# Low-rank weight products as two half-height matmuls side by side, a gate spread in rounded parts, and a few moved instructions

## What is computed

```python
mod = (silu(c) @ wmod).reshape(2, 6, 1, 512)
sa, ca, ga, sb, cb, gb = (mod[:, i] for i in range(6))
ga, gb = (sign(g) * maximum(abs(g), 0.25) for g in (ga, gb))
h = layernorm(x) * (1 + ca) + sa
x = x + ga * (h @ (weight * block_mask).T + bias)
h = layernorm(x) * (1 + cb) + sb
lin = lambda v, w, a, b: v @ w.T + (v @ a.T) @ b.T * 2.0     # rank 16
g = silu(lin(h, w1, A1, B1)) * lin(h, w3, A3, B3)            # hidden 1376
x = x + gb * lin(g, w2, A2, B2)
```

## Time and profile before

| | |
|---|---|
| time, median of 3 runs | 249.12 us (248.8 to 249.45) |
| the profiled execution: its time, its span | 249.18 us, 247.4 us |
| granted TensorE clock, mean | 0.999 of full |
| busy: PE, DVE, ACT, POOL | 239.4, 150.2, 94.6, 40.6 us |

### The profile page before, as it was taken

How to read it: one execution, slowest core, us unless ns; L and a number is a source line. 1 busy time by engine, 2 the same in 40 slices (tenths; PEclk the granted TensorE clock), 3 DMA queues, 4 the chain that set the end, 5 groups by cost and what they waited for, 6 DMA issues and landing times.

```text
span 247.4 us, 3423 instructions
## 1 busy us (share of the span) xinstructions
PE 239.4 (97%) x1205; PEld 187.3 (76%) x1205; DVE 150.2 (61%) x258; ACT 94.6 (38%) x174; POOL 40.6 (16%) x57
## 2 busy tenths in 40 slices
PE   7899899999999999999999999999999999999993
PEld 5567566777778888888888778888888888888772
DVE  2778699989989768855654514745454245424524
ACT  2365388957443231646456212113121212122210
POOL 2002477412101033033032000340000000000000
PEclk9999999999999999999999999999999999999999
DMA  5999999502242342231233550040000000000005
GB/s 132 367 400 389 389 404 388 172 28 85 96 132 71 86 120 53 86 124 44 87 115 65 46 33 0 17 153 3 0 1 0 0 3 0 0 0 3 0 0 170
DMA packets 14565, 26.37 MB, mean 107 GB/s; under 512 B 1618, under 2 KB 3538, under 8 KB 14420
## 3 DMA queue, kind: packets, MB, share of 16 engines
q1 hardware_dynamic: 14112, 26.01, 33.2%
q10 hardware_dynamic: 436, 0.15, 0.2%
HBM read 23.26 MB, written 2.10 MB: 103 GB/s over the span
## 4 chain that ended last, share of the span: by engine, by line
PE 84%; DVE 8%; DMA 2%; issue 1%; ACT 1%; POOL 0%; SPq 0%; DVEq 0%; POOLq 0%; ACTq 0%
PE up_a L1346 17%; PE up_b L1346 16%; PE acc L1372 8%; PE up_a L1355 8%; PE acc L1374 8%; PE acc L1373 8%; PE up_b L1355 8%; PE acc L1300 3%; DMA wa<-in_weight 2%; PE side L1328 2%; DVE stats L816 2%; PE side L1300 2%; DVE wa_lo L918 1%; DVE xt L1006 1%; PE side L1333 1%
## 5 line engine op out<-in xcount | busy, mean ns | idle before, releaser
L1095 DVE TENSOR_TENSOR g<-up_b,g 128x512 f32<-128x512 f32 (+1 forms) x22 | 15.2, 690 | 43.2 <-PE up_b L1355 43.2
L1372 PE MATMUL acc<-w_hi,g_hi 128*128 128x512 f32 (+1 forms) x88 | 34.9, 397 | 0.0
L1374 PE MATMUL acc<-w_hi,g_lo 128*128 128x512 f32 (+1 forms) x88 | 34.8, 395 | 0.0
L1373 PE MATMUL acc<-w_lo,g_hi 128*128 128x512 f32 (+1 forms) x88 | 34.7, 395 | 0.0
L791 ACT ACTIVATE g_hi<-g 128x512 fp32r<-128x512 f32 (+1 forms) x22 | 13.9, 632 | 51.2 <-DVE g L1095 51.2
L976 DVE SCALAR_TENSOR_TENSOR raw<-side,raw 128x512 f32<-128x512 f32 (+2 forms) x31 | 20.2, 677 | 19.1 <-PE side L1328 11.4
L722 ACT ACTIVATE w_hi<-raw 128x512 fp32r<-128x512 f32 (+2 forms) x33 | 20.3, 625 | 17.2 <-DVE raw L976 17.2
L781 ACT ACTIVATE g<-up_a 128x512 f32<-128x512 f32 (+1 forms) x22 | 13.1, 597 | 33.0 <-PE up_a L1355 33.0
L1346 PE MATMUL up_a<-ht_hi,w_hi 128*128 128x512 f32 (+1 forms) x88 | 24.7, 401 | 0.3 <-ACT w_hi L722 0.3
L1346 PE MATMUL up_b<-ht_hi,w_hi 128*128 128x512 f32 (+1 forms) x88 | 23.8, 393 | 0.0
L1355 PE MATMUL up_b<-ht_lo,w_hi 128*128 128x512 f32 (+1 forms) x88 | 23.8, 392 | 0.0
(11 more groups left out here) (162 smaller groups left out, 340.6 us busy)
## 6 DMA issues: line engine op xcount, KB each, us to landing
raw<-in_ffn SPq DMA_DIRECT2D x33, 256.0 KB, 2.7
xt<-in_x SPq DMA_DIRECT2D x8, 256.0 KB, 10.8
wmod_sb<-in_wmod SPq DMA_DIRECT2D x2, 1024.0 KB, 13.8
wmod_sb<-in_wmod SPq DMA_DIRECT2D x1, 2048.0 KB, 14.6
out<-xt SPq DMA_DIRECT2D x8, 256.0 KB, 2.5
mask_sb<-in_mask SPq DMA_DIRECT2D x4, 256.0 KB, 6.5
ca_sb<-in_wmod_ca SPq DMA_DIRECT2D x4, 256.0 KB, 6.4
wa<-in_weight SPq DMA_DIRECT2D x4, 256.0 KB, 6.7
```

The lines of the kernel that those rows point to most:

```text
L1095: nc.vector.tensor_tensor(g[0:w], up_b[0:w], g[0:w], ALU.mult).then_inc(g_ready, 1)
L1372: nc.tensor.matmul(acc[t][:], hi, down_hi[j][0:w], start=(j == 0), stop=False)
L1373: nc.tensor.matmul(acc[t][:], hi, down_lo[j][0:w], start=False, stop=False)
L1374: last = nc.tensor.matmul(acc[t][:], lo, down_hi[j][0:w], start=False, stop=(j == HT - 1))
```

## The change

It has four parts.

1. An up piece is now one weight over all features. `merge_up(j)` issues eight matmuls for a slice: for each of four feature slices k one over rows 0 to 63 of `parts` (w1) and one over rows 64 to 127 (w3), 128 columns each, into two banks. `spread`, `b13` and `half_on` are gone. `up_high(s, n)` waits for piece n alone.
2. The gate of batch 0 stands in two rows of each group (`c` is sent with a third row that repeats the first). ACT rounds the gates (`gate_high`), DVE turns the second row into the remainder (`gate_split`), and `spread_gate` is four single-pass matmuls with `select`.
3. DVE's `columns_sa` stands ahead of `masked_weight_low(1, 2)`. On POOL `x_low(1)` stands ahead of the first `root`; `x_low(2)` and `x_low(3)` wait for the gates instead of `norm_cols_ready`.
4. On PE `spread_gate`, `mod_rows_f` and `columns_f` stand two matmuls (`attend` of one k and m) later, and the two first merges are one `merge_up(0)` ahead of `attend(1, 3, 0, last_two)`.

```diff
-            def spread(j):
...
-                    nc.gpsimd.tensor_scalar(b13[:, n, 0:w],
-                                            f32(parts[:, LORA_B13 + j * P:LORA_B13 + j * P + w]),
-                                            half_on[:, n:n + 1], None, ALU.mult).then_inc(b13_ready, 1)
...
             x_low(0)
+            x_low(1)
             root(NORM_A[0], slice(0, T))
 
-            pool.wait_ge(norm_cols_ready, 1)
-            for k in range(1, KT):
-                x_low(k)
-            spread(0)
+            pool.wait_ge(gates_ready, 1)
+            x_low(2)
+            x_low(3)
...
+            def gate_high():
+                act.wait_ge(gates_ready, 1)
+                nc.scalar.activation(gate_parts[:], gates_a[:], ACT.Copy).then_inc(gate_high_ready, 1)
...
             row_sum(0)
+            gate_high()
             row_sum(1)
...
+            def gate_split():
+
+                dve.wait_ge(gate_high_ready, 1)
+                nc.vector.scalar_tensor_tensor(gate_parts[:], f32(gate_parts[:]), const[:, KEEP_GATE:KEEP_GATE + 1],
+                                               gates_a[:], ALU.mult, ALU.add).then_inc(gate_parts_ready, 1)
...
+            columns_sa()
             masked_weight_low(1, 2)
...
-            columns_sa()
...
             gates_of(0)
+            gate_split()
             masked_weight_low(1, 3)
...
-                    pe.wait_ge(b13_ready, 2 * (j + 1))
-                    for k in range(KT // 2):
-                        at = LORA_A13 + (n * KT // 2 + k) * P
-                        last = nc.tensor.matmul(dst[:, k * 2 * w:(k + 1) * 2 * w], parts[:, at:at + P],
-                                                b13[:, :, 0:w], start=True, stop=True)
...
+                for k in range(KT):
+                    at = LORA_A13 + k * P
+                    for n in range(2):
+                        rows = slice(n * RANKS, (n + 1) * RANKS)
+                        last = nc.tensor.matmul(merge_bank(PIECE[j, n])[:, k * w:(k + 1) * w], parts[rows, at:at + P],
+                                                parts[rows, b:b + w], start=True, stop=True)
+                        if k == KT - 1:
+                            last.then_inc(merge_out, 1)
...
-                pe.wait_ge(w_high_ready, PIECE[j, 1] + 1)
+                pe.wait_ge(w_high_ready, PIECE[j, n] + 1)
...
+            attend(1, 3, 0, first)
             spread_gate()
-            attend(1, 3, 0, first)
...
-            for at in pieces_up(s):
-                merge(PIECE[at])
+                if pieces_up(s):
+                    merge_up(s + 1)
```

More of the change, by code:

```diff
@@ L318, in build @@
         x1_by_dve = sem("x1_by_dve")
-        b13_ready = sem("b13_ready")
         merge_out = sem("merge_out")
@@ L1182, in columns_ca @@
                     pe.wait_ge(ca_ready, k)
-                nc.tensor.matmul(acc[2][:, k * B:(k + 1) * B], mod_rows[:, 0:P], ct[:, KT], start=True, stop=True
+                nc.tensor.matmul(acc[2][:, k * B:(k + 1) * B], mod_rows[:, 0:P], ct[:, KT, 0:B], start=True, stop=True
                                  ).then_inc(ca_cols_out, 1)
@@ new lines, in merge_up @@
+                    for n in range(2):
+                        free_side(("merge", PIECE[j, n]))
+                pe.wait_ge(parts_ready, 2 if j < 2 else 3)
+                b = LORA_B13 + j * P
+                for k in range(KT):
+                    at = LORA_A13 + k * P
+                    for n in range(2):
+                        rows = slice(n * RANKS, (n + 1) * RANKS)
[3 more added lines that the diff above has]
+                            last.then_inc(merge_out, 1)
@@ L1336, in up_high, with merge_down @@
+            def merge_down(r):
+                j, _ = PIECES[r]
+                w = WIDTH[j]
+                free_side(("merge", r))
+                pe.wait_ge(parts_ready, 4 if j < 2 else len(LORA_CUTS))
+                at, b2 = LORA_A2 + (j // 2) * P, LORA_B2 + j % 2 * D
+                nc.tensor.matmul(merge_bank(r)[0:w], parts[:, at:at + w], parts[:, b2:b2 + D], start=True, stop=True
+                                 ).then_inc(merge_out, 1)
             def up_high(s, n, dst):
@@ L1354, in up_rest @@
                         pe.wait_ge(low_by_dve, k + 1)
-                    last = nc.tensor.matmul(dst[0:w], up_hi[j][:, k, n], ht_lo[b][:, k],
+                    last = nc.tensor.matmul(dst[0:w], up_hi[j][:, n, k], ht_lo[b][:, k],
                                             start=False, stop=(k == KT - 1))
@@ L1424, in _ @@
                 attend(1, 0, m, last_two)
+            attend(1, 1, 0, last_two)
             mod_rows_f()
-            for m in range(3):
+            for m in range(1, 3):
                 attend(1, 1, m, last_two)
+            attend(1, 2, 0, last_two)
             columns_f()
-            pe.wait_ge(parts_ready, 2)
-            merge(0)
-            for m in range(3):
+            for m in range(1, 3):
                 attend(1, 2, m, last_two)
+            merge_up(0)
             attend(1, 3, 0, last_two)
-            merge(1)
             attend(1, 3, 1, last_two)
@@ L1462, in _ @@
                         down(0, t)
-                    merge(PIECE[piece_mid(s)])
+                    merge_down(PIECE[piece_mid(s)])
                 if s:
@@ L1472, in _ @@
                 elif s == 1:
-                    merge(PIECE[piece_late(s)])
+                    merge_down(PIECE[piece_late(s)])
                 else:
@@ L1492, in launch_inputs @@
     for j, w in enumerate(WIDTH):
-        both = np.stack([by_feature(up[j * P:j * P + w].T) for up in (w1, w3)], axis=2)
+        both = np.stack([by_feature(up[j * P:j * P + w].T) for up in (w1, w3)], axis=1)
         for n in range(2):
@@ L1514, in launch_inputs @@
     consts[:, KEEP_A] = -(p // R % 2)
-    for n in range(2):
-        consts[:, HALF_ON + n] = p // RANKS == n
     for q in range(KT):
-        consts[q * QUAD, SELECT + q] = 1.0
+        consts[[q * QUAD, q * QUAD + B], SELECT + q] = 1.0
+        consts[q * QUAD + B, KEEP_GATE] = -1.0
     for t in range(T):
```

76 lines of the change are left out of this document (26 added, 50 removed).

## The result

| | before | after |
|---|---|---|
| median | 249.26 us (248.8 to 249.45, 4 runs) | 253.66 us (253.58 to 254.59, 4 runs) |
| profiled execution | 249.18 us, span 247.4 | 254.59 us, span 252.8, mean granted clock 0.989 |
| first `up_a` matmul of the feed-forward part | 48.96 us | 50.24 us |
| from there, steps 0 to 9 | 91.69 us | 94.75 us |
| steps 10 to 20 | 91.62 us | 92.66 us |

The changed kernel is slower: 1.0187 times the time of before [1.0173, 1.0202], 4.4 us by the medians. I had forecast 252.2 us, slower with 0.89. A step here is the time from its first `up_a` matmul to that of the next step; kernels with the same feed-forward code agree in it within some 0.02 us, so it is the ruler of what follows.

A forecast was written before the change was run, and what follows sets the result against it. PE was taken to set the pace over 192 of the 247 us. 249.18 + 3.3 (merges) - 0.27 (wait) + 0 (front) gave 252.2 us, with a range of 248.6 to 254.0 us.

The forecast's parts named there:

- The merge: Up merges on PE: eight half-height matmuls take 0.80 us against 0.47, +0.33 us a slice, +3.3 us for ten.
- the array isn't emptied: Rival: half-height matmuls run among full-height ones without gaps; a merge is 0.44 us, total 248.6 us; 10%.
- the loads don't overlap: Rival: the halves' weight loads don't overlap, or each pair is emptied; 4.4 us more in all, 256.6 us; 10%.
- The 0.27 us wait: Step 1 on PE: the wait for ACT's second rounding goes, as up(1, 0) needs only the first; -0.27 us.
- 0.43 us of 192 are not busy: Feed-forward part on PE: so little idle time that no other wait of the 0.27 us size stands there.
- Those of batch 1 as before: Feed-forward steps: each of batch 0 longer by 0.33 us, those of batch 1 unchanged.
- The front: Ahead of the feed-forward part: gates 1.4 us earlier, but given back behind x_low, attn_gate unchanged; 0 us (-0.7 to +1.3).
- gain nothing: Front on PE: the shorter spread saves nothing, because attend matmuls at 37.18 need attn_gate's second result, at 37.19.
- the front really opens: Rival: DVE isn't held behind x_low, 0.7 to 1.4 us of the gates' lead reach the end; about 251.2 us; 8%.
- the +1.3 of my bounds: Front's upper bound: x_low(1), 1.3 us long, might block DVE's statistics ahead of columns_sa; +1.3 us.

The follow-up runs named there:

- after put back: The changed kernel with an unread tile of 8 bytes, which puts its weight tiles back on multiples of 64 bytes: 251.97 us.
- doubling: after put back with the eight half-height matmuls of each slice issued twice in one visit: 257.05 us.
- splitting: after put back with DVE's last masked-weight residual moved earlier, and merge_up in two visits of two pairs each for all slices but one: 256.36 us.
- the merges alone: The kernel before with only the half-height merges and the weight tiles ordered by weight, front unchanged: 253.52 us.

## Why the prediction came out as it did

The direction and the cause were right; the profiled runs split the 5.43 us of span so (after put back stands between the two):

| term | forecast | measured, us |
|---|---|---|
| ten merges and the waits beside them, steps 0 to 9, tiles in place | +3.3 - 0.27 = +3.03 | +2.42 |
| pace of `up`, steps 0 to 9, then steps 10 to 20 | not named | +0.64, +1.04 |
| front, to the first `up_a` matmul | 0 (-0.7 to +1.3) | +1.28 |
| end | 0 | +0.04 |

That 253.66 us lies inside the range of 248.6 to 254.0 is in part luck: the range above 252.2 us was meant for a dearer merge or a later front, and what carried the median there is a pace that no term had. With the tiles put back it is 251.97 us, close to 252.2, but there a term for the merges and their waits 0.6 us too large and a front some 0.3 later than forecast make up for each other in part.

**The merge, right.** With the tiles in place a step from 3 to 9 is 0.30 to 0.35 us longer, mean 0.325, forecast 0.33. The late entry (0.10 us), the two halves side by side, the 0.20 us from the last pair to the next full-height matmul and the late exit (0.11) all show in the starts, and doubling and splitting confirm the two parts of the price, 0.36 us a visit and 0.11 a pair. That the array is emptied stays the reading of these gaps. The rivals *the array isn't emptied* and *the loads don't overlap* are out. The Trainium skill (TensorEngine Tiling, Theoretical Speedup) gives at most twice the speed for 64 rows and fewer; by that estimate the merge would have been 0.24 us. The trace, with 0.80 on the forecast's count (0.10 + 0.59 + 0.11), decides.

**The waits, right in place, short in size.** The 0.27 us wait is gone. But two more small ones were swallowed by the longer merge: step 0 got 0.26 us shorter instead of 0.06 longer, and step 2 grew by 0.04 instead of 0.33. In step 0, `gate_rows` started 0.54 us behind the last `up_b` matmul before and 0.32 now; in step 2 the first `down` behind the merge came 0.30 us after it before, 0.18 more than the `up_b` matmul behind the merge of step 0. My argument that "0.43 us of 192 are not busy" missed them, because a PE that is busy by its records can still start late.

**"Those of batch 1 as before", wrong.** It is the step that failed. The removal of `b13` and `half_on` was costed as POOL's work alone; that it moves the tiles behind them wasn't looked at. The weight tiles landed 32 bytes off a multiple of 64, and the `up` matmuls went from 229.6 to 233.3 ns: 1.68 us, more than the miss of 1.46 between forecast and median.

**The front, right on DVE, wrong on PE.** `attn_gate` did not move, as worked out. But what I called PE's savings that "gain nothing" made PE arrive at `attend_end` before `uv_split`, which stands behind the held residual: a wait of 1.26 us. Alone it hardly moves the end (39.69 against 39.55 us, and the merges alone, with `merge_up(0)`, already make it 39.80); the fall of the clock that may follow costs 1.0 to 1.5. The medians hold little of it: 4.40 - 2.42 - 1.68 leaves some 0.3. The rival *the front really opens* had a point too: with the residual moved out of `x_low`'s way, `attn_gate` comes earlier and the front gains 0.6 us.

On POOL and DVE, the rows of after show what none of before did, statistics on DVE beside `x_low(1)`:

```profile
25.12 0.68 DVE L800 BATCH_NORM_STATS2 stats<-xt 128x6 f32<-128x512 f32 x1
25.93 0.67 DVE L800 BATCH_NORM_STATS2 stats<-xt 128x6 f32<-128x512 f32 x1
25.17 1.30 POOL L521 TENSOR_TENSOR ht_lo<-raw,ht_hi 128x512 fp32r<-128x512 f32 x1 [1.33 <-ACT ht_hi L595]
```

They take 0.68 and 0.67 us, and 0.68 at 24.31 us without it, so the +1.3 of my bounds did not come from there. The Trainium skill (SBUF, Who interferes with whom) says that a VectorE instruction with a single SBUF input does not contend with GpSimd, outside modes that use two ports; these rows agree.

## What to carry to other kernels

Half-height matmuls side by side lost here: a visit costs 0.36 us beside its pairs, and a pair of 128 columns takes 0.11 us, hardly less than the 0.12 of the full-height matmul of 256 columns that it replaces (0.47 for four). So a longer visit would not pay either: doubled, it is 0.80 + 0.45 = 1.25 us, where twice the four full-height ones would be 0.94 by estimate. Pairs with more columns were not run. When a tile is removed, look at where the tiles behind it now start: 32 bytes cost 1.7 us here, most of it in steps that the edit never touched. And where a saving lets an engine run ahead, find the next thing that it will wait for; a wait that costs nothing by itself may cost its clock.

## What the hardware did that was not expected

- The `up` matmuls (128 x 128 stationary, 512 columns) start 229.5 to 229.6 ns apart with both operands on multiples of 64 bytes in a partition and 233.1 to 233.3 ns with either one 32 bytes off; `down` has 233.4 to 233.6 in every case.
- Two half-height streams ran side by side whatever their order in the program: 14 ns between the halves' starts with four matmuls of the other half ahead.
- The same wait of 1.26 us was followed by half clock in three profiled runs (3.5 us of it in the changed kernel) and by full clock in another.
